# A gated cross-attention network in four stages on one core: the norm's guess ahead of the probabilities' copy on ScalarE, filling products of TensorE left out, GpSimd's memsets first

## The reference

```python
x = x + tanh(g_xattn[0]) * L0_xattn(layernorm(x), ctx)   # stage A, the first cross attention
x = x + tanh(g_ffn[0])   * L0_moe_ffn(layernorm(x))      # stage B
x = x + tanh(g_xattn[1]) * L1_xattn(layernorm(x), ctx)   # stage C
x = x + tanh(g_ffn[1])   * L1_lut_ffn(layernorm(x))      # stage D

# stage A, 16 heads of 16 features; of the 64 context rows 48 are "main", 16 are "dca"
q = ln16(x @ Wq + bq);  k = ln16(y @ Wk + bk);  v = y @ Wv + bv      # ln16: norm over a head
ctx = softmax(q @ k.T / 4) @ v        # over the 48 main rows
ctx = ctx + softmax(q @ kd.T / 4) @ vd  # over the 16 dca rows, with weights of their own
out = ctx @ Wo + bo
```

## Time and profile before

| | before |
|---|---|
| median of 3 runs | 431.32 us (430.88 to 431.6) |
| time of the profiled execution | 430.63 us, its span 428.8 us |
| busy, share of the span | PE 92%, PEld 86%, DVE 72%, ACT 45%, POOL 39% |
| instructions | PE 3664 products and 3664 weight loads, DVE 706, ACT 398, POOL 208 |
| mean granted clock of TensorE | 0.988 of full speed |
| stage A | from the start to about 102 us; its scores begin at 26.48, 45.41, 64.00 and 81.28 us |

### The profile page before, as it was taken

How to read it: one execution, slowest core, us unless ns; L and a number is a source line. 1 busy time by engine, 2 the same in 40 slices (tenths; PEclk the granted TensorE clock), 3 DMA queues, 4 the chain that set the end, 5 groups by cost and what they waited for, 6 DMA issues and landing times. The chain is left out here.

```text
span 428.8 us, 9098 instructions
## 1 busy us (share of the span) xinstructions
PE 393.9 (92%) x3664; PEld 367.9 (86%) x3664; DVE 310.3 (72%) x706; ACT 192.7 (45%) x398; POOL 168.0 (39%) x208
## 2 busy tenths in 40 slices
PE   1889899889998999999899999999999998699995
PEld 0767788779898999999799899989999998699995
DVE  4886778644867768686658998898899789736642
ACT  3556565632442433424355535663554555133331
POOL 3255438240130231312345347545534754233322
PEclk9989999999999999999999999999999999789999
DMA  7502012030003030030200020001001000000000
GB/s 236 172 2 73 27 52 75 3 124 2 2 0 124 2 125 0 2 122 2 65 14 0 2 65 0 2 9 56 2 2 53 2 2 2 0 0 26 27 26 24
DMA packets 6957, 16.33 MB, mean 38 GB/s; under 512 B 1138, under 2 KB 4723, under 8 KB 6404
## 3 DMA queue, kind: packets, MB, share of 16 engines
q1 hardware_dynamic: 6916, 15.75, 11.0%
HBM read 14.70 MB, written 1.05 MB: 37 GB/s over the span
## 5 line engine op out<-in xcount | busy, mean ns | idle before, releaser
L1501 POOL TENSOR_SCALAR work<-work,lut_step,lut 128x344 f32<-128x344 int32 (+1 forms) x60 | 41.9, 711 | 55.1 <-DVE work L1428 53.5
L309 PE MATMUL ps<-wB_hi,workr 128*128 128x256 f32 x224 | 52.6, 298 | 6.0 <-POOL workr L1656 4.6
L309 PE MATMUL ps<-xT_hi,wB_hi 128*128 128x256 f32 x176 | 51.9, 295 | 0.3 <-DVE work L1015 0.3
L1094 POOL TENSOR_TENSOR workr<-work,workr 128x256 fp32r<-128x256 f32 (+1 forms) x36 | 22.9, 636 | 70.2 <-ACT workr L977 70.2
L309 PE MATMUL ps<-xT_lo,wB_hi 128*128 128x256 f32 x176 | 50.3, 286 | 0.0
L309 PE MATMUL ps<-xT_hi,wB_lo 128*128 128x256 f32 x176 | 50.3, 286 | 0.0
L309 PE MATMUL ps<-wN_hi,shared_r 128*128 128x256 f32 x256 | 47.7, 281 | 1.3 <-DVE x L1415 1.3
L309 PEld LDWEIGHTS ps<-wB_hi,workr 128*128 128x128 f32 x224 | 39.4, 194 | 8.1 <-POOL wB_lo L1506 3.8
L1443 DVE COPY_PREDICATED work<-work 128x1376 f32<-128x1376 int32 (+5 forms) x36 | 41.1, 1142 | 2.3
L309 PEld LDWEIGHTS ps<-wN_hi,shared_r 128*128 128x128 f32 x256 | 40.2, 188 | 1.6 <-DVE shared_r L1405 1.4
L309 PE MATMUL ps<-xT_hi,wM_hi 128*128 128x256 f32 x128 | 36.6, 286 | 3.7 <-ACT work L1269 2.3
(11 more groups left out here) (208 smaller groups left out, 1119.1 us busy)
## 6 DMA issues: line engine op xcount, KB each, us to landing
stage<-in_wC SPq DMA_DIRECT2D x4, 1280.0 KB, 5.5
stage<-in_wB SPq DMA_DIRECT2D x4, 768.0 KB, 4.4
stage<-in_idx SPq DMA_DIRECT2D x4, 536.0 KB, 3.4
stage<-in_wA SPq DMA_DIRECT2D x2, 512.0 KB, 5.2
out<-x SPq DMA_DIRECT2D x4, 256.0 KB, 2.1
x<-in_x SPq DMA_DIRECT2D x2, 256.0 KB, 4.3
x<-in_x SPq DMA_DIRECT2D x1, 512.0 KB, 5.3
ctx_n<-in_ctx_n SPq DMA_DIRECT2D x4, 128.0 KB, 2.2
```

The costliest lines, as they stand in the source:

```text
L309: last = nc.tensor.matmul(out, l, r, start=start and i == 0, stop=stop and i == 2)
L1094: nc.gpsimd.tensor_tensor(h_lo[k % 3][0:n], h3[k % 3][0:n], h_hi[k % 3][0:n].bitcast(F32), ALU.subtract).then_inc(*Bp["h_lo"].up())
L1501: nc.gpsimd.tensor_scalar(lev[:, j, 0:n], bits[:, 0, 0:n], lut_step[:, j:j + 1], lut[:, 2 * j:2 * j + 1], ALU.mult, ALU.add).then_inc(*C[" ...
```

## The change

Four edits in stage A, no instruction of another stage is touched.

1. In the three steady groups `act_A_guess` (L447, L449) stands in front of the copy of the probabilities of tile 0 on ScalarE, where it stood behind it.
2. In the steady groups both `keep_warm` calls go, and with the second its wait for `pT_ready`.
3. At the start five filling products stand ahead of the first norm's turn and one behind it, where three and three stood.
4. GpSimd's memsets of `comb_rows` and `sel` stand ahead of its wait for the first variance.

```diff
         def pe_A_start(pe):
             pe.wait_ge(wA_hi_ready, 1)
-            keep_warm(3, 0)
+            keep_warm(5, 0)
             front_pe(pe, 0, FRONT_A)
-            keep_warm(3, 0)
+            keep_warm(1, 0)
...
                 front_pe(pe, g + 2, FRONT_A)
-                keep_warm(5, 0)
             else:
                 keep_warm(12, 4)
             pe_A_probs(pe, g, 0)
...
             pe_A_probs(pe, g, 1)
             if more:
-                pe.wait_ge(*A["pT_ready"].at(g, 1))
-                keep_warm(4, 0)
                 pe_A_turn(pe, n)
...
                 front_upper(act, g + 2, FRONT_A)
+            if more:
+                act_A_guess(act, n)
             act_A_probs(act, g, 0)
             if more:
-                act_A_guess(act, n)
                 act_A_v(act, n)
...
         def pool_A_start(pool):
-            front_pool(pool, 0)
             nc.gpsimd.memset(comb_rows.bitcast(F32), 0.0).then_inc(padded, 1)
             nc.gpsimd.memset(sel.rearrange("p k n -> p (k n)").bitcast(F32), 0.0).then_inc(padded, 1)
+            front_pool(pool, 0)
             front_pool_offset(pool, 1)
```

## The result

In the first series of runs the change made the kernel slower by 1.1%: the median went from 431.1 us (430.7 to 431.6, 4 runs) to **435.4 us** (434.7 to 436.4, 4 runs), ratio 1.011 (95% interval 1.007 to 1.016). My forecast was 426.6 us, its range ended at 429.8, and I had given "slower" 0.08. Ten more executions in a later series (after_again) have a median of 433.1 us against 430.9, but a ratio of 0.999 (0.994 to 1.005). That the kernel after is the slower one is thus clear in the first series alone; that it is not the 1.1% faster that I forecast is clear in both.

What follows compares the result with a forecast made beforehand. Stage A's steady groups were taken as bound by their own order. Start 0.7, group 0 1.9, group 1 2.0 less a 1.9 stop, group 2 2.0: 4.7 us off 431.32 gives 426.6 us, range 424.4 to 429.8.

Steps and rivals of the forecast that it cites:

- The clock: Stage A: rival in which TensorE's clock falls without fillers, each low stretch up to 1.7 us; three or more 0.08.
- my clock case: Stage A: three low stretches, 5.1 us, plus 1.6 us at the start, giving 433.3 us; chance 0.08.
- late rise at the start: Start of stage A: clock rises only behind all twelve k and v products, 1.6 us more than now.
- The stops: Values and scores: TensorE runs out of instructions; 1.9 us lost in group 1, nothing in groups 2 and 3.
- more stops: Rival: groups 2 and 3 lose about 1.0 and up to 1.4 us, 429.0 us; 0.25, shared with low-clock cases.
- bound of 1.85 us for a stop: Values and scores: upper limit of one stop, taken from two packet ends lasting 3.5 us; 1.85 us.
- Stop in group 1: Group 1's scores: a new stop about 8 products in, 1.9 us lost.
- Group 0's stop: Group 0's scores: the present stop of 0.91 us goes along with them.
- The chain: From the turn of tile 0 through guess and copy: scores 2.0 us earlier per steady group, 1.9 in group 0.
- The start: First norm and twelve k and v products come earlier: 0.7 us gained, bounds 1.0 and a loss of 0.9.
- granted clock 1.00 from 33 us on: Sign expected in the profile after: TensorE keeps the higher clock level, 2.4 GHz, from 33 us on.
- three conditions named as making the prediction wrong: Clock falls in a steady group, group 1's scores run through, or a stop stands in group 2 or 3.

Runs made afterwards that it cites:

- guess_only: Kernel before with only the guess moved ahead of the copy of tile 0 on ScalarE; median 430.8 us against 430.9, ratio 0.999.
- after_fill: Kernel after plus four filling products behind group 0's scores and five behind group 3's; median 428.3 us against 430.9 before, ratio 0.993.
- fillers_even: Kernel before without the steady groups' fillers, its 18 start fillers cut into 56 of 164 columns; median 432.8 us (2 runs) against 433.0.
- after_fill_last: Kernel after plus five filling products behind group 3's scores only; median 434.4 us against 430.9 before, ratio 1.000.

## Why the prediction was wrong, step by step

- **The clock is the step that failed most.** In the sum it stood at nothing: I made it a rival with 0.08, "against it" that values and scores ran once at 80.75 without a filler and kept 1.00. The first profile has 21.25 us more at the lower level, some 7.0 us; by the ten executions of after_again the clock costs 4.6. One execution was taken for a rule: guess_only has the same list on TensorE, and its clock falls 3.6 us behind the start of the same scores (79.67; low from 83.25). Of the nine traces with no stop in this burst and no filling products right behind it the clock falls in seven, within 6 us of the start of these scores, and before is one of the two in which it doesn't.
- **Stops and clock were priced as separate rivals.** In groups 1 and 2 every low stretch stands behind a stop. What the prediction lacked is this link, and not only the filling products.
- The sum of my clock case (433.3) lies between the two medians measured, and that is luck: it holds a late rise at the start (1.6), which didn't come, and no stop in groups 2 and 3, where they came.
- The Trainium skill ("TensorE: Matmul & The Clock Gate", Why this matters for your kernels) asks for no idle gaps between bursts. It had pointed the right way, and after_fill agrees with the direction: filling products in two places, nine in all, go with a mean clock of 0.984 in place of 0.972 and a median 4.7 us lower. The gaps here (0.95 us behind the scores of group 0, stops up to 2.65) are shorter than those of which the page speaks, so no run here bears out its figure.
- **The stops are the second step that failed. In groups 2 and 3: "nothing"; measured 2.52 and 0.79.** An end 15 instructions ahead of the values counts, as do 23 (after_fill, 2.18). In the kernel before one 20 ahead did not, nor one 14 ahead of group 3's values in after_fill. My rival "more stops" had priced the two at 1.0 and 1.4, both too far from the truth. The bound of 1.85 us for a stop doesn't hold either: 2.52 here, 2.65 in fillers_even.
- **Stop in group 1: 1.9; measured 1.38**, at the counted product. Group 0's stop stayed (1.01), as I said. All stops: 2.8 forecast (0.9 + 1.9), 5.7 in the first profile and 5.1 in after_again.
- **The chain: 2.0 for each group, 1.9 in group 0; measured 1.73** (15.55 against 17.28) and 1.74 in group 0 (after_fill_last, 25.18 to 41.22, against 17.78). In group 2 the values start 4.86 us behind the turn of tile 0, where I had 4.65. L508 stands behind L280, and L447 0.03 us behind the end of L473, as forecast.
- **The start: 0.7; measured 1.1** (25.38 against 26.48). L250 takes 0.73 us for two, the twelve products 3.46 in place of 3.85. The upper bound of 1.0 was a little low; the late rise didn't come. (The lower bound is off by itself: twelve products 0.95 us earlier and 1.6 longer lose 0.6, not 0.9.)
- What fell with the trace: "granted clock 1.00 from 33 us on", and of the three conditions named as making the prediction wrong two were met, the clock's fall in a steady group and a stop in group 2 or 3. The scores of group 1 did not run through.

## What to carry to other kernels

Before filling products are taken out, read the granted clock of several executions, not of one: a stretch that kept the clock in one trace may lose it in the next, and a mean clock 0.014 lower cost 4.6 us by the estimate above, nearly all of what three groups shortened by 1.7 us each gained. Look at the stops together with the clock: in this kernel removing either the stops or the thin places brought the mean clock back to that of the kernel before. Put the filling products where the engine waits anyway (here behind the scores) instead of ahead of work that others wait for. And where bursts of very short instructions stop with no releaser, count the instructions from the list's start: a few instructions more or fewer far ahead move the stop or remove it.

## What the runs showed of the hardware that I had not expected

- A semaphore increment on TensorE takes about 0.155 us in a row: 120 more of them move the first product from 16.18 to 34.71 us.
- Filling products of few columns cost more than their columns: 56 of 164 took 6.38 us (0.114 each), 18 of 512 take 4.27.
- In stage A the stretches at the lower clock lasted some 3.5 or some 7.0 us in all traces.
- Where a packet of instructions ends in the values, the scores or the filling products behind them, shortly behind another end, TensorE can stop, for 0.27 to 2.65 us in 28 stops of 16 traces. Not every such place has one. The queue "instruction" moves the same 29 packets in every kernel but the one with 220 increments (30).
